# Where an rsqrt's first operations, a chain of adapters and their last steps stand in a fused feed-forward and adapter kernel

## The reference

```python
# first layer, x is (32, 256, 256), cond (32, 64)
scale = cond @ norm_w.T + 1.0
h = x * (scale[:, None, :] * rsqrt(mean(x * x, -1) + 1e-6))
val, gate = split(h @ up_w.T, 2, axis=-1)          # 1024 columns each
h = val * gelu(gate)
hq = round(h * s) / s,  s = 127 / max|h| of each row # int8 rounding
y = hq @ ternary(down_w).T + x                     # y is x of the second layer
# second layer: an adapter whose weights depend on the batch
Wd_b = Wd + 0.1 * (cond @ Wdd.T + bdd).reshape(32, 128, 256)
Wu_b = Wu + 0.1 * (cond @ Wdu.T + bdu).reshape(32, 256, 128)
down = relu(einsum('bld,bnd->bln', y, Wd_b) + bd)
out = y + einsum('bln,bdn->bld', down, Wu_b) + bu
```

## Time and profile before

| | |
|---|---|
| three runs | 521.31, 525.67, 526.25 us; median 525.67 |
| the profiled execution | 522.1 us, of which the span is 520.3 |
| mean granted TensorE clock | 0.978 of full speed |
| busy: PE, PEld, DVE, ACT, POOL | 468.8 (90%), 263.2 (51%), 403.8 (78%), 365.0 (70%), 227.2 (44%) us |
| DMA | 71.64 MB moved, mean 138 GB/s |

### The profile page before, as it was taken

One profiled execution on the slowest core, in us unless ns is written; L12 is line 12 of the kernel. 1 busy time (PEld: TensorE's weight loads), 2 busy tenths in 40 slices (PEclk: granted clock), 3 DMA queues, 4 the chain that ended last, 5 costly groups with the idle time before them and its releaser, 6 DMA issues. The chain is left out here.

```text
span 520.3 us, 9822 instructions
## 1 busy us (share of the span) xinstructions
PE 468.8 (90%) x3206; PEld 263.2 (51%) x3206; DVE 403.8 (78%) x832; ACT 365.0 (70%) x632; POOL 227.2 (44%) x569
## 2 busy tenths in 40 slices
PE   2677988898898999999999999999999999999863
PEld 1234554454555545555555555555555555555442
DVE  3589889998998778778778768877877778887731
ACT  4579777976886777776776877767777666677631
POOL 0164245325433126546445445445454444444355
PEclk9999999998999999999999999999999999999957
DMA  7856866585552444555565545565555446553442
GB/s 249 331 103 197 191 189 156 160 225 177 149 162 59 87 100 104 120 141 130 130 136 131 126 111 131 142 122 132 137 97 143 108 107 113 122 122 72 102 116 76
DMA packets 120402, 71.64 MB, mean 138 GB/s; under 512 B 104672, under 2 KB 105376, under 8 KB 118176
## 3 DMA queue, kind: packets, MB, share of 16 engines
q1 hardware_dynamic: 120352, 71.02, 54.3%
HBM read 37.44 MB, written 8.39 MB: 88 GB/s over the span
## 5 line engine op out<-in xcount | busy, mean ns | idle before, releaser
L674 PE MATMUL bank<-up_hi,xs_hi 128*128 128x512 f16 x512 | 154.0, 383 | 11.3 <-DVE hid L555 6.0
L414 ACT ACTIVATE gel<-bank,rms 128x512 f32<-128x512 f32 x128 | 87.2, 682 | 98.7 <-PE bank L674 89.9
L674 PE MATMUL bank<-up_hi,xs_lo 128*128 128x512 f16 x512 | 153.7, 382 | 0.0
L674 PE MATMUL bank<-up_lo,xs_hi 128*128 128x512 f16 x512 | 153.7, 382 | 0.0
L555 DVE SCALAR_TENSOR_TENSOR hid<-bank,rms,gel 128x512 f32<-128x512 f32 x128 | 95.4, 745 | 15.8 <-ACT gel L414 14.9
L419 ACT ACTIVATE hid<-hid,amax 128x1024 f32<-128x1024 f32 x64 | 73.2, 1144 | 26.3 <-DVE amax L569 26.1
L350 POOL TENSOR_TENSOR ad_lo<-adapt,ad_hi 128x256 f16<-128x256 f32 x64 | 41.6, 670 | 110.4 <-DVE ad_hi L601 110.4
L674 PEld LDWEIGHTS bank<-up_lo,xs_hi 128*128 128x128 f16 x512 | 50.4, 98 | 61.6 <-issue 2.1
L674 PEld LDWEIGHTS bank<-up_hi,xs_lo 128*128 128x128 f16 x512 | 50.4, 98 | 61.4 <-issue 1.6
L563 DVE TENSOR_REDUCE amax<-hid 128x1 f32<-128x1024 f32 x64 | 78.1, 1220 | 2.2
L674 PEld LDWEIGHTS bank<-up_hi,xs_hi 128*128 128x128 f16 x512 | 48.6, 99 | 48.7 <-issue 12.5
(11 more groups left out here) (65 smaller groups left out, 629.0 us busy)
## 6 DMA issues: line engine op xcount, KB each, us to landing
xT_s<-in_xT SPq DMA_DIRECT2D x32, 256.0 KB, 3.1
xn_s<-in_xn SPq DMA_DIRECT2D x32, 256.0 KB, 3.2
stage<-in_WddT SPq DMA_DIRECT2D x8, 1024.0 KB, 6.1
stage<-in_WduT SPq DMA_DIRECT2D x8, 1024.0 KB, 5.1
out<-out_s SPq DMA_DIRECT2D x32, 256.0 KB, 2.4
adapt<-in_up_wT SPq DMA_DIRECT2D x4, 512.0 KB, 6.3
x<-in_down_wT SPq DMA_DIRECT2D x1, 1024.0 KB, 12.7
qT<-qn SPq DMA_TRANSPOSE x64, 3.1
```

Source lines behind the costliest of these rows:

```text
L414: nc.scalar.activation(gel[:, c], u_gate[c][:], ACT.Gelu, scale=rms[:, t // TPB % XN_SLOTS, t % TPB:t % TPB + 1]).then_inc(gelu_done, 1)
L674: ins = nc.tensor.matmul(dst[:], a[:, t // TPB % 2, k, cols], w[:, c, k, v, :], start=(k == 0 and n == 0), stop=(k == KD - 1 and n == 2))
```

## The change

1. VectorE's `rsqrt_guess` moves from the start of an odd step to behind gate product, residual, total and evacuations (in step 1, where there is nothing to evacuate, still ahead of the ternary conversion of the down weights).
2. ADAPT[b] becomes the larger of 2b + 7 and 19 + (4b + 2) // 3, and the last three batches stand at 64, 65 and 67. So in the first stretch three batches come in four steps (before: two in three), from batch 20 on each stands three steps earlier than before. The steps end at NT + 6 = 70.
3. A tile is split at the earliest in step t + 3, where its residual sum is made. From step 40 on that is so for each tile.
4. In step NT on ScalarE the cast of tile 61 comes ahead of `quantize` of tile 63.

```diff
-END = NT + 9
+END = NT + 6

 def adapter_step(b):

-    if b >= B - 4:
-        return (NT + 1, NT + 2, NT + 3, NT + 5)[b - B + 4]
-    return max(2 * b + 10, NGEN + 4 + (3 * b + 1) // 2)
+    if b >= B - 3:
+        return (NT, NT + 1, NT + 3)[b - B + 3]
+    return max(2 * b + 7, NGEN + 3 + (4 * b + 2) // 3)

 def split_tiles(s):

-    return [2 * b + i for b in range(B) for i in range(TPB) if ADAPT[b] - 4 + i == s]
+    return [t for t in range(NT) if max(ADAPT[t // TPB] - 4 + t % TPB, t + DOWN) == s]
...
                 if s < NT:
                     gelu(s, 0)
-                if 0 <= s - 1 < NT:
-                    quantize(s - 1)
+                    if s > 0:
+                        quantize(s - 1)
                 for t in split_tiles(s):
                     residual_high(t)
+                if s == NT:
+                    quantize(s - 1)
                 if 0 <= s - 1 < NT:
                     quantized(s - 1)
...
             for s in range(END):
-                if s % TPB == 1 and s // TPB + 1 < B:
-                    rsqrt_guess(s // TPB + 1)
                 if s < NT:
                     gate(s, 0)
...
                 if 2 <= s < NGEN + 2:
                     evacuate(s - 2, 0)
                     evacuate(s - 2, 1)
+                if s % TPB == 1 and s // TPB + 1 < B:
+                    rsqrt_guess(s // TPB + 1)
                 if s == 1:
                     ternary()
```

## The result

The changed kernel took 527.63 us (median of 19 runs, 526.13 to 530.23), the kernel before 525.21 beside it (19 runs, 521.31 to 526.75). The ratio is 1.0053, with a 95% interval of 1.0034 to 1.0072. The forecast was 520.1. The time lies inside the range of 512 to 529 and is 0.5% up, less than the 1% that the prediction counts as no change, but it moved up where a fall was forecast. The profiled execution took 527.7 (before: 522.1), with a span of 525.8 (520.3): +5.5 in the span, against the forecast's -5.6.

A forecast was written before the change was run, and what follows sets the result against it. Generation was taken as bound by a four-engine loop, later steps by TensorE, the tail by waits. Terms -7.6, +2.6, +5.4 and -6.0 sum to -5.6: 516.5 from the profiled 522.1, 520.1 from the median 525.67; range 512 to 529.

The forecast's parts named there:

- Generation: Steps 1 to 16: moving the guess cuts two steps from 17.59 to 16.6 us; with the steps around, -7.6 us.
- T + 0.94: Odd generation steps: the moved L543 starts 0.94 us after the generation's start T, no longer held by GpSimd's low part.
- The rival without a hold: Generation: small GpSimd rsqrt operations aren't held by VectorE's low part; periods of 15.9, -12.3 us, 515.4; chance 0.20.
- some 1.3 stay: After step 15: nothing is generated two steps on, so some 1.3 us of TensorE's 1.69 wait stay gained.
- Outside this stage L543 is held 0.47: Outside generation: the guess is held 0.47 us or not at all; moved, it costs no more than VectorE's slack.
- the rsqrt becomes the bound: Generation: the rsqrt's later start costs more than the held operations show; periods of 17.2, 523.5 us; chance 0.18.
- the cast's loop with more holds: From step 40: more GpSimd holds on VectorE make two steps 15.3 us, +18.2, 532.9 in all; chance 0.12.
- Denser adapters: By the GELU of step 39: two middles and two outputs more, moved work of +2.6 us, given back in the tail.
- The waits that come closer: GpSimd's wait for the store of two batches before and SyncE's queued transposes: more than half a step kept, no cost.
- The cast, three steps closer: Steps 40 on: the cast waits for VectorE's residual sum; two steps go from 13.78 to 14.23 us, +5.4 in all.
- The loop that I worked out: Steps 40 on: a ScalarE and VectorE loop through the cast, 6.16 plus 7.77, 13.93 us a pair without holds.
- The tail: From the last GELU to the end: 24.7 us against 30.7, -6.0, with the last transpose deciding.

The follow-up runs named there:

- e13: The changed kernel again, unaltered: 525.38 us, ratio 1.0013 to the kernel before.
- e2: The kernel before with rsqrt_guess moved behind the evacuations throughout and nothing else: 518.51 us, ratio 0.9888.
- e5: The changed kernel with the guess first in the odd step again from step 18 on and splits one step later except the last eight tiles: 511.14 us.
- e4: The changed kernel with each tile split one step later, at the earliest in step t + 4, except the last eight tiles: 522.40 us.
- e1: The changed kernel with the guess behind the evacuations in generation only, first in the odd step from step 18 on: 516.30 us.
- e3: The changed kernel with the guess first in the odd step throughout, so only adapters, splits and last steps are new: 528.15 us.
- e9: The changed kernel with ScalarE quantizing tile 63 ahead of the cast of tile 61 in step 64, as before: 523.47 us.
- e6: The kernel before with the guess moved behind the evacuations in the generation's steps only: 511.53 us, ratio 0.9747.
- e14: The changed kernel with one wait more: GpSimd's low part of chunk 1 waits for VectorE's: 525.85 us.
- e15: The changed kernel with one wait more: VectorE's low part of chunk 1 waits for GpSimd's: 528.23 us.

## Why the prediction was wrong

**Generation: right.** Forecast 16.6 a period, measured 16.35, and for the reason given: L545 free and where it was put (T + 0.94 forecast, T + 0.98 measured), one rsqrt operation held by the low part (1.08), the GELU ended by the rsqrt. The rival without a hold is out. Of the 8.3 in steps 3 to 16, some 1.7 came by a way that the forecast doesn't have: one period of before took 19.27 and not 17.6, with the granted clock at 0.91 around it. In step 1 the forecast had 0.5 and no tie; in the profile of after nothing came of it, in e13 2.5. The Trainium skill (page "SBUF — State Buffer", section "SBUF: two separate sides") says that of a GpSimd operation and a VectorE one with two SBUF inputs whichever starts first has the pair of ports for its whole instruction. The 1.08 here and the hold of 1.5 in the race of step 1 agree with it. The records of e13 and of the earlier trace rows, where the operation recorded 0.02 us ahead is the one held, don't, unless they can't tell starts as close as that apart. (Of the 2.34 that the prediction calls holding in the earlier trace rows, 0.16 is the operation itself.) Of the gain after step 15, where "some 1.3 stay", nothing came: steps 16 to 18 lost 1.4, and GELU 0 of step 18 waits 4.1 for the late rsqrt.

**The step that failed** is in the same part: "Outside this stage L543 is held 0.47 ... or not at all; behind the gate product it costs no more than VectorE's slack." I priced the three operations at their own length on VectorE and did not follow their result. The chain is guess, 3.2 to 3.6 us of GpSimd, GELU 0 of the next step, and it has its own slack, which VectorE's doesn't show. Before, L543 was first in the odd step, the result was there 0.4 to 1.5 ahead of the GELU, and the GELU waited for TensorE, 89.9 of 98.7 us (as at 107.90 and 111.34 in the earlier trace rows). The move takes 2.3 from that slack: GpSimd idles 3.63 for the guess and the GELU 2.65 for GpSimd. Priced by runs: 4.4 in steps 18 to 40 alone (e2), 6.3 on top of the denser adapters. I had the mechanism in hand, "the rsqrt becomes the bound", with "only 1.4 us to spare", but as a rival for generation alone, where it was already the bound in my own forecast. Taken through the 22 steps from 18 to 40, at the 4.4 to 6.3 that the runs show, it would have brought the sum from -5.6 to about zero. That the time still lies inside the range is luck: its upper part was there for the cast's loop with more holds, which didn't come.

**Denser adapters: half.** Moved work was forecast at 2.6, measured at 2.9. "The waits that come closer ... keep more than half a step by my count" was false for the store: in steps 18 to 40 1.8 us of waits in the changed kernel, where the late guess covers them, and 7.7 in e5, worth 2.0. And the work comes back earlier than the tail: steps 40 to 62 of e5 take 1.1 less than before.

**The cast, three steps closer: right in size, wrong in make.** Forecast 14.23 a pair, measured 14.26 for steady pairs, +5.7 in all. But in the changed kernel the loop that closes is the other one. Its timeline in the late steps:

```profile
436.12 0.67 ACT L414 ACTIVATE gel<-bank,rms 128x512 f32<-128x512 f32 x1
...
441.04 0.74 DVE L557 SCALAR_TENSOR_TENSOR hid<-bank,rms,gel 128x512 f32<-128x512 f32 x1
...
442.99 0.16 DVE L545 TENSOR_SCALAR nwt<-ssum 128x2 f32<-128x2 f32 x1
443.51 0.37 POOL L332 TENSOR_TENSOR nwt<-nwt 128x2 f32<-128x2 f32 x1 [7.41 <-DVE nwt L550]
...
446.90 0.69 ACT L414 ACTIVATE gel<-bank,rms 128x512 f32<-128x512 f32 x1 [1.72 <-POOL rms L343]
...
449.11 0.40 ACT L434 CAST x1n<-x 128x256 f16<-128x256 f32 x1 [0.48 <-DVE x L586]
```

Gate product, residual, total, guess, rsqrt, GELU 0: the cast waits only 0.48, behind a GELU that waited 1.72, and behind the cast comes GELU 1 (as at 436.12), for which VectorE's queue waits. So it is one loop, of which the cast's 0.48 is a link; without it (e4) the shortest pairs take 13.78 and not 14.26. The loop that I worked out stands bare in e1, where the guess is early:

```profile
425.48 0.67 ACT L414 ACTIVATE gel<-bank,rms 128x512 f32<-128x512 f32 x1
...
432.21 0.41 ACT L434 CAST x1n<-x 128x256 f16<-128x256 f32 x1 [0.87 <-DVE x L586]
433.49 0.67 ACT L414 ACTIVATE gel<-bank,rms 128x512 f32<-128x512 f32 x1
...
439.68 0.67 ACT L414 ACTIVATE gel<-bank,rms 128x512 f32<-128x512 f32 x1
```

Its halves are 8.01 and 6.19 (forecast 7.77 and 6.16), a pair of 14.05 on average over steps 40 to 62. So the cast's loop is real, and worth 5.3 of these steps (e1 against e5; from before to e3 it is 4.2, with the 1.1 of moved work); the rsqrt's loop, on average 14.01 a pair without the casts' waits (e4), stands beside it, and only e5, with neither, is at 13.57.

**The tail: near,** -5.3 for a forecast of -6.0 (by e13's profile -3.5). The transpose of tile 63's quantized rows and down 63, after:

```profile
504.53 0.40 ACT L434 CAST x1n<-x 128x256 f16<-128x256 f32 x1 [2.73 <-DVE x L586]
504.84 1.14 ACT L419 ACTIVATE hid<-hid,amax 128x1024 f32<-128x1024 f32 x1
...
512.32 1.91 PE L686 MATMUL bank<-tern,qT 128*128 128x256 bf16 x8
...
515.84 1.22 SPq L272 DMA_TRANSPOSE x1T<-x1n  x1
...
518.34 0.38 PE L714 MATMUL bank<-x1T,ad_hi 128*128 128x256 f16 x2 [2.68 <-issue]
```

The last middle now starts at 518.34, behind a transpose issued at 515.84, and 7.5 before the end, so the last transpose does decide, as forecast. What I took for granted is the new order of step 64: the cast waits 2.73 with the quantizing behind it, and e9 shows that this costs 1.5 to 2 rather than gains.

## What to carry to other kernels

Before moving an operation to the end of a step, follow its result to the engine that consumes it and write down the slack of that whole chain; the slack of the engine that it runs on says nothing of it. A move that gains in one stage can be confined to the stage: e6 is the kernel before with one condition and takes 2.5% less, where the whole change gains nothing. When undoing either of two parts gives little, undo both: two loops of nearly one length hide each other.

## What the runs showed of the hardware

- Two operations that want the same ports and start 0.02 to 0.04 us apart can go either way in one and the same program (after and e13); with either order forced the medians are 2.4 us apart (e14, e15), and by their times whole sets of runs fell on one side or the other. By the records the one that starts first isn't always the winner: in e13 GpSimd's is recorded 0.02 ahead and is the one held, as in the earlier trace rows.
- GpSimd operations of only 2 columns are held as well, 1.08 in place of 0.19, by a VectorE operation that is under way.
- From step 3 on, the granted clock fell in generation in both kernels that have the guess first there (before once, e3 twice), and in none of the sixteen profiles that have it behind the evacuations. Before, it stood at 0.50, the lower level of 1.2 GHz, from 122.5 to 125.5 us, and the period took 1.67 longer than its neighbours. Ahead of step 3 it fell in kernels of both kinds (0.91 over 13 to 33 us in e2, e3 and e13). The line of before around the fall:

```profile
113.00:133.00 20.00, 17.64 (x165) 10.02 (x164) 16.93 (x28) 14.93 (x25) 7.33 (x14) 0.91 0.63 173
```

TensorE is busy for 18.45 of the same 20 us in e2, where the clock is 1.00. Before the fall it had stood idle for 1.70 us (from 120.22); but one period earlier it stood idle for 1.69, and the clock stayed at 1.00. So the gaps alone don't decide it, and what does wasn't found.
